# Differential attention: the values of four heads projected at once, token tiles stationary and 512 weight columns moving, with transfers and splits of their own

## The reference

```python
q = (x @ Wq)...; k = (x @ Wk)...; v = (x @ Wv)...       # per head, 128 wide
scores1 = q1 @ k1 * SCALE; scores2 = q2 @ k2 * SCALE      # halves of 64, causal
diff_attn = softmax(scores1) - lam * softmax(scores2)     # lam = sigmoid(lambda_init) of the head
out = diff_attn @ v
return concat_heads(out) @ Wo
```

## Time and profile before

| | |
|---|---|
| runs | 997.39, 1002.46, 1004.04 us; median 1002.46 |
| profiled execution | 1003.17 us, its span 1001.3 us (1.9 us lie around the span) |
| mean granted TensorE clock | 0.868 of full |
| busy share of the span | TensorE 88%, DVE 62%, ACT 43%, POOL 37% |
| chain that ended last | TensorE 72%, DVE 16%, issue 4%, ACT 3%, POOL 2%, DMA 2% |

### The profile page before, as it was taken

One profiled execution on the slowest core, in us unless ns is written; L12 is line 12 of the kernel. 1 busy time (PEld: TensorE's weight loads), 2 busy tenths in 40 slices (PEclk: granted clock), 3 DMA queues, 4 the chain that ended last, 5 costly groups with the idle time before them and its releaser, 6 DMA issues.

```text
span 1001.3 us, 17358 instructions
## 1 busy us (share of the span) xinstructions
PE 878.2 (88%) x6128; PEld 713.9 (71%) x6128; DVE 615.9 (62%) x987; ACT 431.0 (43%) x738; POOL 369.8 (37%) x350
## 2 busy tenths in 40 slices
PE   6378886799999689799869999987998699999997
PEld 5233233689888578588648999966887588888886
DVE  5979886465566547668746666435666444445444
ACT  2368775143443235345424555411222244545452
POOL 2145655133323224278532334211221234444442
PEclk9755555799999879789957999977999689999999
DMA  4057775021111113112100100110110022333331
GB/s 165 0 108 150 154 148 116 17 64 64 48 57 47 43 48 95 32 58 63 52 0 17 32 31 31 33 47 22 43 42 26 27 80 83 94 93 95 85 95 53
DMA packets 102531, 64.02 MB, mean 64 GB/s; under 512 B 71761, under 2 KB 90705, under 8 KB 102354
## 3 DMA queue, kind: packets, MB, share of 16 engines
q1 hardware_dynamic: 102482, 63.37, 23.6%
HBM read 46.05 MB, written 0.52 MB: 47 GB/s over the span
## 4 chain that ended last, share of the span: by engine, by line
PE 72%; DVE 16%; issue 4%; ACT 3%; POOL 2%; DMA 2%; SPq 0%; DVEq 0%; POOLq 0%; ACTq 0%
PE ps L153 18%; PE ps L155 16%; PE ps L154 16%; PE ps L1283 6%; DVE nm L790 3%; PE ps L552 2%; PE ps L1561 2%; PE ps L865 2%; PE ps L1562 2%; PE ps L1262 2%; DVE soft L1737 1%; POOL vf L607 1%; PE ps L876 1%; PE ps L314 1%; PE ps L1580 1%
## 5 line engine op out<-in xcount | busy, mean ns | idle before, releaser
L215 POOL TENSOR_TENSOR wa_lo<-raw,wa_hi 128x512 fp32r<-128x512 f32 (+2 forms) x112 | 147.2, 1314 | 173.9 <-ACT wa_hi L206 171.0
L215 POOL TENSOR_TENSOR wb_lo<-raw,wb_hi 128x256 fp32r<-128x256 f32 (+1 forms) x112 | 92.2, 823 | 287.2 <-ACT wb_hi L206 287.2
L153 PE MATMUL ps<-xt_hi,wa_hi 128*128 128x512 f32 x352 | 147.6, 419 | 6.8 <-DVE xt_lo L278 4.4
L155 PE MATMUL ps<-xt_hi,wa_lo 128*128 128x512 f32 x352 | 143.8, 408 | 0.0
L154 PE MATMUL ps<-xt_lo,wa_hi 128*128 128x512 f32 x352 | 143.7, 408 | 0.0
L669 ACT ACTIVATE kres<-ps,nb,qs 128x1024 int16<-128x1024 f32 x64 | 77.1, 1205 | 29.9 <-DVE nb L795 26.3
L1107 DVE TENSOR_TENSOR hh<-sg,ps 128x512 f32<-128x512 f32 x56 | 38.5, 688 | 77.2 <-PE ps L155 71.9
L153 PEld LDWEIGHTS ps<-xt_hi,wa_hi 128*128 128x128 f32 x352 | 69.4, 197 | 22.6 <-issue 3.8
L1109 DVE TENSOR_TENSOR h_lo<-hh,h_hi 128x512 fp32r<-128x512 f32 x56 | 59.3, 1060 | 41.7 <-ACT h_hi L1099 41.7
L607 POOL CAST vf<-pti 128x1024 bf16<-128x1024 int16 x64 | 66.3, 1042 | 49.3 <-DMA pti<-kres 47.1
L790 DVE TENSOR_REDUCE nm<-ps 128x1 f32<-128x1024 f32 x64 | 77.9, 1218 | 10.2 <-PE ps L552 9.8
(11 more groups left out here) (255 smaller groups left out, 2051.5 us busy)
## 6 DMA issues: line engine op xcount, KB each, us to landing
raw<-w_l1f SPq DMA_DIRECT2D x44, 256.0 KB, 2.7
raw<-w_l0a SPq DMA_DIRECT2D x16, 384.0 KB, 3.3
raw<-w_l1f SPq DMA_DIRECT2D x44, 128.0 KB, 2.0
raw<-w_l1p SPq DMA_DIRECT2D x32, 128.0 KB, 2.1
raw<-w_l1x SPq DMA_DIRECT2D x32, 128.0 KB, 2.1
raw<-w_l1a SPq DMA_DIRECT2D x16, 256.0 KB, 2.9
raw<-w_l0f SPq DMA_DIRECT2D x12, 256.0 KB, 2.7
raw<-w_l0a SPq DMA_DIRECT2D x16, 128.0 KB, 2.3
```

Source lines behind the costliest of these rows:

```text
L153: nc.tensor.matmul(o, a[0], b[0], start=start, stop=False, **kw)
L155: return nc.tensor.matmul(o, a[1], b[0], start=False, stop=stop, **kw)
L215: nc.gpsimd.tensor_tensor(lo[:, u, 0:w], raw[:, u, cols], hi[:, u, 0:w].bitcast(F32), ALU.subtract).then_inc(done, 1)
```

## The change

The values of four heads (a group, `VG` = 4) are projected together: for each of the four token tiles, 2 feature halves x 3 = 6 matmuls, the token tile stationary and 512 weight columns moving, into one bank. That is 24 matmuls for four heads, against 96 before. One tile of the next group is made per head: tile h % 4 of group h // 4 + 1 in heads 0 to 11, behind the scores; all four tiles of group 0 stand in head 0, ahead of the scores, in banks 2 to 5. Heads 12 to 15 have none.

- The a part of a block shrinks from 768 to 512 columns (q and k). The value columns have transfers of their own (`load_values`, two of 256 KB per group, in pieces of 512 bytes) into `wv_raw`, a hi split on ACT (`value_hi`) and a lo split on POOL (`value_lo`) of 1024 columns each, into two buffers `wv`. `vh` holds two groups.
- SyncE: group 0 ahead of the transpositions of the cross attention, once `q_rep` and `k_rep` are made; group 1 behind them; group 2 between b of block 3 and a of block 4, group 3 between b of block 7 and a of block 8. In this stage a(n) waits for the a split of n-2, as before.
- ACT: hi of a(0) and the values' hi of group 0 move ahead of the last evictions of the cross attention; a(1) and the values' hi of group 1 behind the layer norm. In head h ACT makes hi of b(h-1) and then hi of a(h+2), where it was a(h+1); in heads 3 and 7 the values' hi of groups 2 and 3 follow, ahead of `turned`.
- POOL: b(h), a(h+2) in its loop as before, and the values' lo of group h // 4 + 2 behind them for h = 3 and 7 (so in TensorE's heads 4 and 8).
- TensorE: the scores follow the k projection with only the two transposes between; `a_used` is now signalled by the k projection. PV waits for the group's copies (`ve`), as does the first turn.
- DVE: the copy of a value tile moves behind the subtraction of the maximum; from group 2 on it waits for PV of the group before the last.
- The loops over heads are written out on TensorE, ACT, DVE, POOL and SyncE. Two pairs of semaphores are merged (`kz` into `idbf`, `acc0` and `nqk` into `set`).

The diff, cut to its core:

```diff
-L0A = (0, 16, 768, 256)
+L0A = (0, 16, 512, 256)
+VG = 4
...
+        def load_values(sp, g):
+            if g:
+                sp.wait_ge(wv_lo, g)
+            heads = w_l0a[VG * g:VG * (g + 1), :, 4 * P:6 * P].rearrange("a p (c d) -> c p a d", c=C2)
+            for c in range(C2):
+                sp.dma_start(wv_raw[:, c, :].rearrange("p (a d) -> p a d", a=VG), heads[c]).then_inc(wv_loaded, 16)
+
+        def load_heads(sp):
+            load_values(sp, 1)
+            for n in range(2, H):
+                if n % VG == 0 and n // VG + 1 < H // VG:
+                    load_values(sp, n // VG + 1)
+                load_block(sp, n, n % 2, n, w_l0a, L0A, 2 * P)
...
@@ l0x_pool_units
+            lo_part(pool, "a", 0, L0A[0], L0A)
+            value_lo(pool, 0)
@@ l0x_act
+            hi_part(act, "a", 0, L0A[0], L0A)
+            value_hi(act, 0)
...
+        def l0a_values(pe, g, t, bank):
+            n = VG * g + t
+            pe.wait_ge(wv_lo, g + 1)
+            if n >= VG:
+                pe.wait_ge(l0["ve"], n)
+            for c in range(C2):
+                last = mm3(ps[:, bank, :], xt(c, t * P, P), wv_of(g, c), c == 0, c == 1)
+            last.then_inc(l0["v"], 1)
@@ l0a_project
-                last.then_inc(l0[name], 1)
-            if exists(h, h - 1):
-                pe.wait_ge(l0["ve"], h)
-            for t in range(NT):
-                for c in range(C2):
-                    last = mm3(ps[:, 2, t * P:(t + 1) * P], xt(c, t * P, P), wa(u, 4 * P + c * P, P), c == 0, c == 1)
-            last.then_inc(a_used, 1)
+                last.then_inc(l0[name] if k == 0 else a_used, 1)
@@ l0a_pe_head
+            if h == 0:
+                for t in range(NT):
+                    l0a_values(pe, 0, t, 2 + t)
             ...
             l0a_scores(pe, h, u)
+            if h + VG < H:
+                l0a_values(pe, h // VG + 1, h % VG, 2)
@@ l0a_pool
-            lo_parts(pool, L0A, L0F, 2)
+            value_lo(pool, 1)
+            for h in range(H):
+                lo_part(pool, "b", 0, N1 + h, L0A)
+                if h + 2 < H:
+                    lo_part(pool, "a", 0, N1 + h + 2, L0A)
+                if h % VG == 3 and h // VG + 2 < H // VG:
+                    value_lo(pool, h // VG + 2)
+            lo_part(pool, "a", 0, N1 + H, L0F)
@@ l0a_act, head
-                next_part(hi_part, act, i, u, L0A, None)
+                if h + 2 < H:
+                    hi_part(act, "a", 0, N1 + h + 2, L0A)
+                if h % VG == 3 and h // VG + 2 < H // VG:
+                    value_hi(act, h // VG + 2)
@@ l0a_dve
+            def values(g, t, bank):
+                dve.wait_ge(l0["v"], VG * g + t + 1)
+                if g >= 2:
+                    dve.wait_ge(l0["pv"], VG * (g - 1))
+                nc.vector.tensor_copy(vh[:, g % 2, t, :, :].rearrange("p a d -> p (a d)"), ps[:, bank, :]).then_inc(l0["ve"], 1)
```

More of the change, by code:

```diff
@@ L170, in apart, with load_block @@
             eng.sem_inc(passed_pool if eng is nc.gpsimd else passed_pe, 1)
-        def load_block(sp, n, k, m, src, stage):
+        def load_block(sp, n, k, m, src, stage, skip=0, first=False):
             u, a, cols = k % 2, stage[2], stage[2] + stage[3]
@@ L178, in load_block @@
                 sp.wait_ge(a_split, n - 1)
-                if isinstance(n, int):
+                if first:
                     sp.wait_ge(b_split, n - 1)
@@ L858, in l0a_pv @@
             pe.wait_ge(l0["te"], h + 1)
+            pe.wait_ge(l0["ve"], VG * (h // VG + 1))
             if exists(h, h - 1):
@@ L864, in l0a_pv @@
                 k0 = T * (b % 2)
-                last = nc.tensor.matmul(ps[:, 4 + b % 2, (b // 2) * T:(b // 2 + 1) * T], vh[k0:k0 + T, u, b // 2, :], ddt[k0:k0 + T, g // 2, T * p:T * (p + 1)], start=True, stop=True)
+                last = nc.tensor.matmul(ps[:, 4 + b % 2, (b // 2) * T:(b // 2 + 1) * T], vh[k0:k0 + T, h // VG % 2, b // 2, h % VG, :], ddt[k0:k0 + T, g // 2, T * p:T * (p + 1)], start=True, stop=True)
             last.then_inc(l0["pv"], 1)
@@ L898, in l0a_pe @@
             pe.wait_ge(ln_lo, 4)
[L899 to L903, removed]
+            for h in range(H):
+                l0a_pe_head(pe, h)
             l0a_turn(pe, H - 1, 1)
@@ L907, in l0a_pe, with value_lo, value_hi @@
             l0a_out(pe, H - 1, 1, final=True)
+        def value_lo(pool, g):
+            pool.wait_ge(wv_hi, g + 1)
+            nc.gpsimd.tensor_tensor(flat(wv[:, g % 2, 1]), flat(wv_raw[:]), flat(wv[:, g % 2, 0]).bitcast(F32), ALU.subtract).then_inc(wv_lo, 1)
         def l0a_pool(pool):
-            lo_part(pool, "a", 0, L0A[0], L0A)
             ln_pool(pool, 1)
             lo_part(pool, "a", 0, L0A[0] + 1, L0A)
-            lo_parts(pool, L0A, L0F, 2)
+            value_lo(pool, 1)
+            for h in range(H):
+                lo_part(pool, "b", 0, N1 + h, L0A)
[4 more added lines that the diff above has]
+            lo_part(pool, "a", 0, N1 + H, L0F)
+        def value_hi(act, g):
+            act.wait_ge(wv_loaded, 32 * (g + 1))
+            if g >= 2:
+                act.wait_ge(l0["v"], VG * (g - 1))
+            nc.scalar.activation(flat(wv[:, g % 2, 0]), flat(wv_raw[:]), ACT.Copy).then_inc(wv_hi, 1)
         def l0a_act(act):
-            hi_part(act, "a", 0, L0A[0], L0A)
             ln_act(act, 1)
+            hi_part(act, "a", 0, N1 + 1, L0A)
+            value_hi(act, 1)
             nc.scalar.activation(flat(wl_hi[:]), flat(wl[:]), ACT.Copy).then_inc(la["whi"], 1)
@@ L926, in after @@
                 act.wait_ge(l0["pv"], h + 1)
[L927 removed]
+                if h >= 2:
                     act.wait_ge(b_used, h + N1 - 1)
                 nc.scalar.activation(by_batch(ot_hi[:, u, 0, :]), banks45(), ACT.Copy).then_inc(l0["ohi"], 1)
[L931 to L932 removed]
+            for h in range(H):
+                u = h % 2
                 act.wait_ge(l0["q"], h + 1)
[L934 removed]
+                if h >= 1:
                     act.wait_ge(l0["s"], h)
                 nc.scalar.activation(qh[:], ps[:, 0, :], ACT.Copy).then_inc(l0["qe"], 1)
[L937 removed]
+                act.wait_ge(a_used, N1 + h + 1)
                 nc.scalar.activation(kh[:], ps[:, 1, :], ACT.Copy).then_inc(l0["ke"], 1)
[L939 to L942 removed]
+                if h >= 1:
+                    hi_part(act, "b", 0, N1 + h - 1, L0A)
+                if h + 2 < H:
+                    hi_part(act, "a", 0, N1 + h + 2, L0A)
+                if h % VG == 3 and h // VG + 2 < H // VG:
+                    value_hi(act, h // VG + 2)
+                if h >= 1:
                     turned(h - 1)
@@ L945, in head @@
                 nc.scalar.activation(pr[:, u, :], st, ACT.Exp, scale=T ** -0.5).then_inc(l0["e"], 1)
-                if exists(h, h - 1):
+                if h >= 1:
                     after(h - 1, 1 - u)
[L949 to L957, removed]
             hi_part(act, "b", 0, N1 + H - 1, L0A)
+            hi_part(act, "a", 0, N1 + H, L0F)
             turned(H - 1)
@@ L1006, in head @@
                 nc.vector.tensor_tensor(dd[:, u, :], pr[:, u, 0:256], pr[:, u, 256:512], ALU.add).then_inc(l0["d"], 1)
-                if exists(h, h - 1):
+                if h >= 1:
                     after(h - 1, 1 - u)
[L1010 to L1014, removed]
+            for h in range(H):
+                head(h, h % 2)
             after(H - 1, 1)
@@ L1359, in l1x_pool @@
             lo_part(pool, "b", 0, NP, L1P)
-            nc.gpsimd.memset(acc[:], 0.0).then_inc(l1["acc0"], 1)
-            nc.gpsimd.tensor_tensor(nqk[:], vec[:, NQ:NQ + H], vec[:, NK:NK + H], ALU.mult).then_inc(l1["nqk"], 1)
+            nc.gpsimd.memset(acc[:], 0.0).then_inc(l1["set"], 1)
+            nc.gpsimd.tensor_tensor(nqk[:], vec[:, NQ:NQ + H], vec[:, NK:NK + H], ALU.mult).then_inc(l1["set"], 1)
             def proj(i, u):
@@ L1369, in proj @@
                 pool.wait_ge(l1["accq"], m + 1)
-            pool.wait_ge(l1["acc0"], 1)
+            pool.wait_ge(l1["set"], 1)
             for u in range(2):
@@ L1471, in l1x_dve @@
             ln_dve(dve, 3)
-            dve.wait_ge(l1["acc0"], 1)
-            dve.wait_ge(l1["nqk"], 1)
+            dve.wait_ge(l1["set"], 2)
             for u in range(2):
@@ L1825, in _ @@
             for src, stage in zip((w_l0a, w_l0f, w_l1p, w_l1x, w_l1a, w_l1f)[:6], (L0A, L0F, L1P, L1X, L1A, L1F)):
-                load_first(sp, src, stage)
                 if stage is L0A:
+                    load_first(sp, src, stage, 2 * P)
+                    sp.wait_ge(x0["qrep"], 1)
+                    sp.wait_ge(x0["krep"], 2)
+                    load_values(sp, 0)
                     l0x_sync(sp)
-                load_rest(sp, src, stage)
+                    load_heads(sp)
+                else:
+                    load_first(sp, src, stage)
+                    load_rest(sp, src, stage)
             sp.wait_ge(ff["ev"], CH0 - 1 + E1)
```

51 lines of the change are left out of this document (30 added, 21 removed).

## The result

The changed kernel takes 1048.23 us (median of 4 runs, 1039.34 to 1055.59) where the one before took 1001.05 in the same comparison: ratio 1.043, 95% interval 1.0384 to 1.0477. It is slower, by 47 us by the medians and by 4.3% by the ratio. The forecast was 1045 us, in a range of 1018 to 1064. The profiled execution took 1047.88 us, 44.7 more than the profiled one of before.

A forecast was written before the change was run, and what follows sets the result against it. The prediction took TensorE, busy all the time at full clock, to bound the stage. Its terms, 3.6 + 2.6 + 11.6 - 2.1 - 2.1 + 6.6 + 2.1 + 4.7 + 15.2, gave +42.2 us: 1045 us, range 1018 to 1064.

The forecast's parts named there:

- Head 0: First head of the stage: all four value tiles of group 0 added, V projection removed, an earlier wait covered: +3.6 us.
- The uncovered kh: Ahead of the scores: ACT's kh eviction loses the V projection as cover, so TensorE waits 0.55 us in each head.
- the wait for the load: Heads 1 to 13: ACT's earlier a split waits for its transfer; 10.15 us per head; +2.6 (head 1), +11.6 (heads 2 to 13).
- the value transfers: SyncE, heads 2 and 6: two value transfers between the b and a parts delay the a part, +3.3 us each, +6.6.
- the value splits: ACT's in heads 3 and 7, +2.1 us together; POOL's late lo split in heads 4 and 8, +4.7 for both.
- the clock: TensorE falls to half clock behind idles of 2.7 us or more, in eight heads at 1.9 us: +15.2 us.
- L: Time origin of a head on TensorE: the instant at which its k projection has been issued.
- POOL's value split: Heads 4 and 8: value-lo ends late, TensorE waits 3.95 us; head 12.5 us for 10.15, +4.7 for both.
- The tail: Head 15 and the end of the stage: V projection removed, kh wait added, -2.1 us.
- Rival one: The load is not waited for: 999 us with POOL's late value-lo, 991 without the POOL wait; chance 0.10.
- Rival two: Same waits but no clock loss, value transfers beside the rest: +22 us, 1025 us; chance 0.22.
- Rival three: The clock falls in all heads 1 to 13: +52 us, 1055 us, or 1065 with 2.7 us per head; chance 0.20.

The follow-up runs named there:

- the filled run: Changed kernel plus matmuls of no use, as many as each idle time of TensorE holds, no wait removed: 1033.39 us, ratio 1.0298 to the kernel before.

## Why the prediction was right, point by point

The forecast sum was +42.2 us; the two profiled executions are 44.7 apart. The heads are measured here from one kh eviction to the next.

- Head 0: forecast +3.6; 10.89 us for 7.23, +3.7.
- The uncovered kh: forecast 0.55 us, 0.51 to 0.52 measured in most heads.
- Heads 1 to 13 (the wait for the load, the value transfers, the value splits and the clock together): forecast +42.8 (2.6 + 11.6 + 6.6 + 2.1 + 4.7 + 15.2). Measured 166.25 us in the changed kernel for 7.56 + 12 x 9.18 = 117.7: +48.5.
- Of it, the clock: forecast 15.2, measured 19.8 in the changed kernel's profile. This is the mis-sized term. From the start of PV to the next L a head at full clock takes 3.94 us, and five heads did; the other eight (1, 2, 3, 6, 7, 10, 12, 13) took 1.5 to 3.1 more, 16.5 in sum (PV and what follows it, as in head 13 above). Heads 4 and 8 lost 3.3 more ahead of PV, against the same stretch at full clock in the filled run. The same count in the profile of the repeated changed kernel gives 19.9.
- Two parts of that term were wrong. Head 1 was put among those with 1.6 us of idle; it has no output projection, so by the prediction's own figures it has 3.2 (2.97 measured), and its clock fell. And PV at half clock was taken as 0.5 us more; it costs 0.86 (1.90 us from PV's start to q's in head 13, for 1.04). Where q and k are slow nearly throughout a head loses 3.1 us (12 and 13), and 1.5 in five others, for the 1.9 assumed in each.
- The heads in which the clock falls differ from execution to execution: head 1, with an idle of 2.97 us, took 13.1 us in one profile and, with 2.87, 10.3 in the other. That it falls in just those heads with 2.7 us or more of idle was too sharp.
- The rest: forecast 27.6, by the difference 28.7. It came near because its errors cancel. The a part was issued at L+2.30 and not at L+2.5, and split 2.7 to 3.2 us after its issue, for 2.7 assumed: PV came 1.0 us late in sum over the six heads 1, 3, 7, 9, 11 and 12. In heads 5, 10 and 13 the issue itself took 1.1 to 1.5 us, which nothing in the forecast had: 2.5 us. Against both, the value transfers delayed PV by some 2.2 and 1.7 us in heads 2 and 6, not by 3.3 each.
- POOL's value split: forecast 3.95 us of idle, 3.85 measured. The length forecast for heads 4 and 8 at full clock, 12.5 us, is what the filled run shows (12.50 both times). The run without this wait gave 3.6 us (1044.96 less 1041.39) to 7 us (by the ratios), clock included.
- The value tile: forecast 1.4 us, measured 1.39 for 6 matmuls, 0.23 each. The Trainium skill ("TensorE: Matmul & The Clock Gate", Back-to-back issue gap) has 131 ns; the measurement decides. An estimate from that figure, 6 x 131 ns = 0.79 us, would be 0.6 us too short.
- Head 14: forecast 7.12, measured 7.11. The tail: forecast -2.1; from the last kh to the next layer norm's transposes it is 20.3 us for 22.5, -2.2. The next layer norm's transposes come 47.5 us later than before, 5.3 more than the forecast sum; 2.7 us of it are gained back behind this stage, in parts that the change doesn't touch. No run was aimed at them, and that the total came within 2.5 us is luck to that extent.

Rival one named the price of the schedule without the wait, 999 us with POOL late and 991 without: measured 999.27, 999.31 and 992.28. Rival two (1025, no clock loss) is what the filled run comes near: 1033. It is 8 us above, with five long a issues and value transfers that still cost more than their issues. Rival three (the clock down in all heads) didn't come: the profile has full clock in heads 5, 9 and 11.

So the change itself, 24 matmuls for 96, is a small gain: 1.1% with both waits undone, 2.0% with the value tile moved too. As it was made, it is lost mostly by one index, h + 2 for h + 1 in ACT's split, and for 7 us by POOL's late split.

## What to carry to other kernels

Where transfers are issued by one queue in a fixed order, a split or a copy that is moved a step ahead must be followed back through that queue: here the a part stood behind a b part, whose release hung on the instruction just ahead of the moved one. That one engine is busy 100% of a stage doesn't tell how close the others are; the slack of each is in the timeline and can be priced before the change. And an instruction taken out of a full engine may have been another's cover: put in its place what the change adds.

## What the runs showed that I had not expected

- An issue on SyncE's queue can take about three times its usual length: 1.14 us at 259.84 and 1.54 at 321.26, where 0.43 is usual. In the profiles of the kernel before, the changed one and all the runs, every issue of a weight block of this stage that took over 0.6 us stood 0.37 to 0.53 us behind the issue before it (two that share one row of 7.44 us in the run with a ahead of b can't be told apart). In the other heads of that run, where the two are 1.2 us apart, none took more than 0.52. Why a close second is sometimes slow, no run shows. Where the transfer was needed a head later this cost nothing; in the changed kernel it is on the chain.
- The idle in front of PV is not what decides the clock alone. Head 1 in the changed kernel's profile, then in that of its repeat:

```profile
209.51 1.97 PE L898 MATMUL ps<-ddt,vh 64*128 64x64 f32 x16 [2.97 <-ACT ddt L978]
```

```profile
210.74 1.11 PE L898 MATMUL ps<-ddt,vh 64*128 64x64 f32 x16 [2.87 <-ACT ddt L978]
```

The first was followed by half clock, the second by full clock. In the repeat the clock also fell behind an idle of 1.86 us (head 5).
